# Layer 1 of an eight-expert network by seven block products: a graph-attention and expert-layer kernel in float32

## What is computed

```
x1  = x + gnn(layernorm(x), adj)                       # 128 graphs, softmax over 128 neighbours
xn  = layernorm(x1)
w   = softmax(mean over graphs(xn) @ Wr + br)          # [node, expert]
h   = relu(bn(xn @ W1[e] + b1[e]))                     # 256 x 256 each, bn = scale and shift
h   = relu(bn(h  @ W2[e] + b2[e]))
y   = sum over e of  w[node, e] * (h @ Wo[e] + bo[e])
out = x1 + y
```

## Time and profile before

| | before |
|---|---|
| three runs, us | 2537.67, 2536.6, 2537.84; median 2537.67 |
| span of the profiled execution, us | 2535.1 |
| PE busy, share of the span | 2453.0 us, 97% |
| ACT busy | 1592.8 us, 63% |
| DVE busy | 1479.0 us, 58% |
| POOL busy | 408.1 us, 16% |
| DMA | 116.02 MB, mean 46 GB/s |

### The profile page before, as it was taken

How to read it: one execution, slowest core, us unless ns; L and a number is a source line. 1 busy time by engine, 2 the same in 40 slices (tenths; PEclk the granted TensorE clock), 3 DMA queues, 4 the chain that set the end, 5 groups by cost and what they waited for, 6 DMA issues and landing times.

```text
span 2535.1 us, 38086 instructions
## 1 busy us (share of the span) xinstructions
PE 2453.0 (97%) x14000; PEld 2125.7 (84%) x14000; DVE 1479.0 (58%) x2160; ACT 1592.8 (63%) x2142; POOL 408.1 (16%) x450
## 2 busy tenths in 40 slices
PE   7888789999999999999999999999999999999998
PEld 6666668888888888888888888888888888888887
DVE  6999965555555555555555555555555555555554
ACT  6777746666666666666666666666666666666665
POOL 5888820000000000000000000000000000000000
PEclk9999989999999999999999999999999999999999
DMA  6666510000000000000000000000000000000000
GB/s 190 214 203 202 188 61 26 26 12 13 25 25 25 25 25 25 25 25 25 25 25 25 25 2 22 25 25 25 25 25 25 25 25 25 25 25 25 14 11 25
DMA packets 88991, 116.02 MB, mean 46 GB/s; under 512 B 4572, under 2 KB 76680, under 8 KB 88968
## 3 DMA queue, kind: packets, MB, share of 16 engines
...
## 4 chain that ended last, share of the span: by engine, by line
PE 86%; ACT 0%; DVE 0%; issue 0%
PE ps_wide L158 56%; PE ps_y L1096 28%; PE ps_t L145 1%; ACT h L923 0%; DVE h_lo L1003 0%; DVE h2w L998 0%; ACT h_hi L948 0%; DVE out_sb L1010 0%; ACT h_hi L935 0%; PE ps_t L1112 0%; ACT featT L958 0%; PE ps_t L1107 0%; DVE h_lo L991 0%
## 5 line engine op out<-in xcount | busy, mean ns | idle before, releaser
L923 ACT ACTIVATE h<-ps_wide,bn_cols 128x512 f32<-128x512 f32 x1024 | 791.0, 776 | 494.7 <-PE ps_wide L158 487.4
L991 DVE TENSOR_TENSOR h_lo<-h,h_hi 128x1024 fp32r<-128x1024 f32 x256 | 313.4, 1224 | 604.1 <-ACT h_hi L935 604.1
L1096 PE MATMUL ps_y<-w_hi,h_hi 128*128 128x256 f32 x2048 | 572.2, 279 | 2.2 <-DVE h_lo L1003 2.2
L1096 PE MATMUL ps_y<-w_lo,h_hi 128*128 128x256 f32 x2048 | 571.8, 279 | 0.0
L1096 PE MATMUL ps_y<-w_hi,h_lo 128*128 128x256 f32 x2048 | 570.8, 279 | 0.0
L1003 DVE TENSOR_TENSOR h_lo<-h2w,h_hi 128x1024 fp32r<-128x1024 f32 x256 | 376.5, 1471 | 290.7 <-ACT h_hi L948 290.7
L948 ACT ACTIVATE h_hi<-h2w 128x1024 fp32r<-128x1024 f32 x256 | 271.4, 1060 | 336.5 <-DVE h2w L998 336.5
L158 PE MATMUL ps_wide<-xT_hi,w_hi 128*128 128x512 f32 x1024 | 405.6, 396 | 3.3 <-ACT h L923 3.3
L158 PE MATMUL ps_wide<-h_hi,w_hi 128*128 128x512 f32 x1024 | 407.7, 398 | 0.0
L158 PE MATMUL ps_wide<-xT_lo,w_hi 128*128 128x512 f32 x1024 | 405.8, 396 | 0.0
L158 PE MATMUL ps_wide<-xT_hi,w_lo 128*128 128x512 f32 x1024 | 405.4, 396 | 0.0
...
## 6 DMA issues: line engine op xcount, KB each, us to landing
x_sb<-in_x SPq DMA_DIRECT2D x32, 512.0 KB, 3.5
res<-in_x SPq DMA_DIRECT2D x32, 512.0 KB, 4.5
x_scratch<-x SPq DMA_DIRECT2D x32, 512.0 KB, 3.0
x1t<-x_scratch SPq DMA_DIRECT2D x32, 512.0 KB, 4.5
resb<-x_scratch SPq DMA_DIRECT2D x32, 512.0 KB, 5.2
out<-out_sb SPq DMA_DIRECT2D x32, 512.0 KB, 3.6
...
```

The costliest lines, as they stand in the source:

```text
L923: last = nc.scalar.activation(h[:, c, :], psum[:, c, :], ACT.Relu, bias=bn_cols[:, row + 1, C * e + c:C * e + c + 1], scale=bn_cols[:, row ...
L991: nc.vector.tensor_tensor(h1_lo[p][:, :, :], h1[:, :, :], h1_hi[p][:, :, :].bitcast(F32), ALU.subtract).then_inc(lo1_done, 1)
L1096: mm = nc.tensor.matmul(ps_y[:, b4, :], h[:, c, cols], w[:, i, c, :], start=(e == 0 and n == 0 and b4 % per_bank == 0), stop=(e == E - 1 a ...
```

## The change

Layer 1 is computed by Strassen's scheme, in the form with shared sums: the 256 x 256 weight is four blocks of 128 x 128, x is four blocks of 128 x 256 (two feature halves by two halves of the 512 columns), and instead of eight block products there are seven. Each is three matmuls of 256 columns. Names: a tile's seven x blocks stand in `xs`, `xq_hi`, `xq_lo`, an expert's seven weight blocks in `wq_hi`, `wq_lo`.

- **Weight sums**, in the first stage: POOL makes four sums of 128 columns for an expert and the low part of 896 columns, ACT the high part, one expert in two groups; then W2 one a group. Wo is loaded and split in the second stage, at its start (`wo_hi`, `wo_lo`).
- **x sums**, once a tile: ACT copies the transposed x to `xs` (`tile_copy`), POOL makes four differences (`tile_sums`), and ACT and DVE split the seven blocks in three pieces of 3, 2 and 2 blocks (`tile_high`, `tile_low`).
- **Partial results**: PE accumulates product 1 (`a_sum`); ACT reads it with scale and shift into `v` (v1); PE adds products 4 and 5, ACT reads again (v2); PE adds product 6, ACT reads a third time (v3). DVE adds what the other half of the banks holds: `sum_2` writes z of output half 1 from v3, `sum_1` z of output half 0 from v1 and v2, after product 7. ACT's high part takes relu with it, and DVE's low part is max(z, 0) - high.
- **Order**: a step runs layer 1 of a unit, layer 2 of the unit before, and layer 3 of the unit three back (`LEAD = 3`), interleaved as below. There is one set of h1 parts in place of two, and h2 is gated in place.
- **Statistics kept**: the mean and reciprocal deviation of every group, which the first stage has for the feature mean anyway, stay in `mean_all` and `rstd_all`; the second stage no longer computes them. x is normalised in place in `x1t`.
- **Output**: the residual sum is made in `resb` itself in two halves, so the residual of the next tile is loaded after the store of this one has landed.

The diff, cut to its core:

```diff
+        def tile_copy(act, t, ps_x):
+            act.wait_ge(xT_ready, t + 1)
+            wait(act, xqlo_done, 3 * t)
+            for c, (first, step) in enumerate(((B11, B12 - B11), (B21, B22 - B21))):
+                last = nc.scalar.activation(xs[:, first:first + step + 1:step, :],
+                                            ps_x[:, c, :].rearrange("p (t n) -> p t n", n=H), ACT.Copy)
+            last.then_inc(xs_copied, 1)
+
+        def tile_sums(pool, t):
+            pool.wait_ge(xs_copied, t + 1)
+            nc.gpsimd.tensor_tensor(xs[:, T1, :], xs[:, B12, :], xs[:, B11, :], ALU.subtract).then_inc(xs_sum, 1)
+            nc.gpsimd.tensor_tensor(xs[:, T3, :], xs[:, B22, :], xs[:, B12, :], ALU.subtract).then_inc(xs_sum, 1)
+            pool.wait_ge(xs_sum, 4 * t + 2)
+            nc.gpsimd.tensor_tensor(xs[:, T2, :], xs[:, B22, :], xs[:, T1, :], ALU.subtract).then_inc(xs_sum, 1)
+            pool.wait_ge(xs_sum, 4 * t + 3)
+            nc.gpsimd.tensor_tensor(xs[:, T4, :], xs[:, B21, :], xs[:, T2, :], ALU.subtract).then_inc(xs_sum, 1)
+
+        def tile_high(act, t, group):
+            act.wait_ge(xs_sum, 4 * (t + 1))
+            q = slice(*X_GROUPS[group])
+            nc.scalar.activation(xq_hi[:, q, :], xs[:, q, :], ACT.Copy).then_inc(xqhi_done, 1)
...
-            def steps(t, last):
-                for s in range(1, E + 1):
-                    us = [unit(t, s + 2), unit(t, s + 1), unit(t, s)]
...
             @block.sync
...
+                    wait(sp, out_stored, 16 * t)
                     sp.dma_start(resb[:, :, :].rearrange("p b d -> p (b d)"), x1_dram[t]).then_inc(res_loaded_b, 16)
-                    sp.wait_ge(out_done, t + 1)
-                    sp.dma_start(out_g[t], out_sb[:, :, :]).then_inc(out_stored, 16)
+                    sp.wait_ge(out_done, 2 * (t + 1))
+                    sp.dma_start(out_g[t], resb[:, :, :]).then_inc(out_stored, 16)
...
             @block.scalar
...
+                def step(t, n):
+                    new, prev, old = unit(t, n), unit(t, n - 1), unit(t, n - 2)
+                    if exists_unit(prev):
+                        high_1(prev)
...
+                    if exists_unit(new):
+                        act.wait_ge(p1_done, uno(new) + 1)
+                        wait(act, z1_done, uno(new))
+                        copy_sum(new, 0, 0, v1_done)
+                    if exists_unit(old):
+                        relu_2(old, 1)
+                    if new[1] == E - 1 and exists_unit(unit(t, n + 1)):
+                        act.wait_ge(p2_done, uno(new) + 1)
+                        tile_high(act, unit(t, n + 1)[0], 0)
+                    if exists_unit(new):
+                        act.wait_ge(p4_done, uno(new) + 1)
+                        copy_sum(new, 1, 0, v2_done)
...
+                    if exists_unit(old):
+                        high_2(old)
+                    if new[1] == E - 1 and exists_unit(unit(t, n + 1)):
+                        tile_high(act, unit(t, n + 1)[0], 1)
+                    if exists_unit(new):
+                        act.wait_ge(p7_done, uno(new) + 1)
+                        wait(act, z2_done, uno(new))
+                        copy_sum(new, 2, 1, v3_done)
...
+                    if exists_unit(prev):
+                        relu_2(prev, 0)
+                    if new[1] == E - 2 and exists_unit(unit(t, n + 2)):
+                        tile_copy(act, unit(t, n + 2)[0], ps_t_x)
...
             @block.vector
...
+                def step(t, n):
+                    new, prev, old = unit(t, n), unit(t, n - 1), unit(t, n - 2)
+                    done = unit(t, n - LEAD)
+                    if exists_unit(prev):
+                        low_1(prev)
...
+                    if exists_unit(old):
+                        gate_2(old)
+                    if new[1] == E - 1 and exists_unit(unit(t, n + 1)):
+                        tile_low(dve, unit(t, n + 1)[0], 0)
+                    if done[1] == E - 1 and exists_unit(done):
+                        out_add(done[0], 0)
+                        out_add(done[0], 1)
+                    if exists_unit(new):
+                        sum_2(new)
+                    if exists_unit(old):
+                        low_2(old)
+                    if new[1] == E - 1 and exists_unit(unit(t, n + 1)):
+                        tile_low(dve, unit(t, n + 1)[0], 1)
+                    if exists_unit(new):
+                        sum_1(new)
...
             @block.tensor
...
+                def strassen(out_ps, e, q, start, stop):
+
+                    terms = ((wq_hi, xq_hi), (wq_lo, xq_hi), (wq_hi, xq_lo))
+                    for n, (w, x) in enumerate(terms):
+                        mm = nc.tensor.matmul(out_ps, w[:, e, q, :], x[:, q, :], start=start and n == 0,
+                                              stop=stop and n == len(terms) - 1, skip_group_check=True)
+                    return mm
...
+                        wait(pe, z2_done, uno(new))
+                        strassen(a_sum, e, 0, True, False).then_inc(p1_done, 1)
+                        wait(pe, z1_done, uno(new))
+                        strassen(x_p5, e, 1, True, False)
+                        strassen(x_p2, e, 2, False, False).then_inc(p2_done, 1)
...
+                        layer_3(done, 0)
+                    if exists_unit(new):
+                        pe.wait_ge(v1_done, uno(new) + 1)
...
+                        strassen(a_sum, e, 3, False, False)
+                        strassen(a_p4, e, 4, False, False).then_inc(p4_done, 1)
...
+                    if exists_unit(done):
+                        layer_3(done, 1)
+                    if exists_unit(new):
+                        pe.wait_ge(v2_done, uno(new) + 1)
...
+                        strassen(a_sum, e, 5, False, True).then_inc(p7_done, 1)
+                    if exists_unit(prev):
+                        pe.wait_ge(lo1_done, uno(prev) + 1)
+                        wait(pe, r2_done, C * uno(prev))
+                        layer_2(prev, 0)
+                    if exists_unit(new):
+                        pe.wait_ge(z2_done, uno(new) + 1)
+                        strassen(x_p5, e, 6, False, True).then_inc(p3_done, 1)
+                    if exists_unit(prev):
+                        layer_2(prev, 1)
```

656 lines of the change are left out of this document (347 added, 309 removed).

## The result

| | before | after |
|---|---|---|
| time, median of the runs (us) | 2537.76 | 2699.24 |
| range (us) | 2536.6 to 2538.99 | 2698.47 to 2699.66 |
| span of the profiled execution (us) | 2535.1 | 2697.5 |
| TensorE (PE) busy | 97% | 93% |
| tile in the expert stage (us) | 68.06 | 72.49 |

A forecast was written before the change was run, and what follows sets the result against it. It took PE's own queue to bound the expert stage. Its terms summed to +114 us on a span of 2535.1, so 2649, and 2652 us as the runs' median, 4.5% slower, with a range of 2575 to 2735.

The forecast's parts named there:

- hand-over: Between product 6 and product 7 in each unit: PE waits some 0.2 us for ACT and DVE, +45 us.
- the high ends: Upper bounds of the forecast's terms, which its range up to 2735 us had to take in.
- products: Layer 1 on PE: 21 matmuls of 256 columns replace 12 of 512, 0.35 us less a unit, -90 us.
- product 6 to product 7: Layer 1: ACT's read and DVE's sum outlast half of layer 2 by 0.2 us a unit, +45 us.
- step before a new tile: Once a tile, POOL's differences delay ACT's v2 and PE's products 6 and 7: 3.75 us in 31 tiles, +116 us.
- the piece ahead of the last sum: DVE's piece of x work adds a 0.2 us wait at the next step's second product, +6 us.
- rival 2: PE's clock falls after each tile's 2.9 us gap, 1.7 us lost each time, +54 us, 2706 us; chance 0.2.
- residual: Later residual load makes POOL's bias addition block DVE's low part of layer 2, 0.5 us a tile, +15 us.
- first stage and crossing: POOL's added weight work, +6 us, and a later barrier between the stages, +4 us.
- start of the second stage: First steps: feature mean, gate and third-layer weight splits stand between the hand-overs, +12 us.
- Rival 1: Expert stage: PE stays the bound, a tile takes about 66.9 us, 2523 us in all, faster; chance 0.11.
- rival 3: Expert stage: the loop of DVE and ACT rules every unit at 8.7 us, 2767 us; chance 0.07.

The follow-up runs named there:

- e2: The changed kernel with product 7 behind eight of layer 2's twelve matmuls instead of six: 2650.5 us.
- e12: e11 with DVE's third low piece of x put back behind the second, in the step of expert 7: 2493.4 us.
- e3: The changed kernel with 18 matmuls that nobody reads put ahead of product 6 in the step of expert 7: 2694.2 us.
- e1: The changed kernel with the next tile's normalisation, transposes, ACT's copies and POOL's four differences one step earlier: 2626.3 us.
- e4: e1 with the four differences of x made by DVE instead of POOL, behind its last sum in the step of expert 6: 2598.7 us.
- e5: e4 and e2 together: 2557.9 us.
- e10: e9 with the bias added to the residual by DVE in the step of expert 5 instead of by POOL: 2505.8 us.
- e11: e10 with third-layer weights split one expert a step, eight steps instead of four, and the first residual loaded earlier: 2502.5 us.
- e9: e5 with DVE's later low pieces one place later, and ACT's copies and second piece and DVE's differences moved into idle waits: 2524.9 us.

## Why the prediction was right, and where it was short

The mechanism was right: PE waits for DVE's z ahead of product 7, and once a tile for ACT's v behind POOL's differences. The sum of the terms was +114 us against a span of 2535.1; it came to +162.4. The two largest errors, of PE's own work (21 us) and of the hand-over (24), lie on the same side, so the range holds through the room that it left for the clock and the high ends.

| term, as predicted | predicted | measured | from |
|---|---|---|---|
| products | -90 | -69 | plain step with all waits gone, 8.13 (e2, e12), against 8.40: 0.27 x 256 |
| product 6 to product 7 | +45 | +69 | 8.44 - 8.13 = 0.31, x 224 |
| step before a new tile | +116 | +116 | 11.87 - 8.13 = 3.74, x 31 |
| the piece ahead of the last sum | +6 | +9 | step 0 without low clock 8.73 (e3), less 8.44, x 31 |
| clock (rival 2) | 0 | +7 | 8.94 - 8.73, x 31 |
| residual | +15 | +4 | 8.58 - 8.44, x 31 |
| first stage and crossing | +10 | +5 | 351.49 - 346.80 |
| start of the second stage | +12 | +20 | what is left of 162.4 |
| tail | 0 | +2 | 6.6 - 4.6 |

**Products.** The step "half the columns cost half the time" was wrong by a little, and 256 times over. I took 0.117 us for 256 columns from 24 halves in a row behind 24 whole ones. In a step where 45 of 57 matmuls have 256 columns, 8.13 less 12 times 0.233 leaves 0.1184 for each. That is 0.08 us a unit, 21 us in all. In e12, where nothing waits, it lies with layer 3 as well: its two halves of 12 matmuls take 1.43 us each, 2.86 together, where its 24 in a row took 2.80 before, and the 21 of the products take some 2.49 instead of 2.45. So "nothing else leaves PE" was right, and that what stays keeps its price was not. One half in e12, its first matmul and the product's behind it, 1.43 us apart:

```profile
1252.14 0.28 PE L1201 MATMUL ps_y<-wo_hi,h_hi 128*128 128x256 f32 x1
...
1253.57 0.28 PE L1181 MATMUL ps_wide<-xq_hi,wq_hi 128*128 128x256 f32 x1
```

Why 256-column matmuls are some 1.5% slower in this order was not tried.

**Product 6 to product 7.** Five of the six parts fit: 0.32 from product 6's last matmul to ACT (0.31 charged), 0.60 from there to DVE (0.58). The sum takes 0.75 us and not 0.67; I had taken the fastest of 32 of another line, with both operands in SBUF, where the same row has a median of 1.42; both new sums, the one over two banks of PSUM (L1069, 751 ns on average) and the one over one (L1079, 744), take longer than that. With 0.04 more at the hops and the restart, 0.31 instead of 0.2 us: +24. e2 shows that it is this wait, and that nothing takes its place in a plain step.

**The step before a new tile.** Right in the sum, 3.74 against 3.75, which is in part luck: the forecast's own parts, 2.9 to 3.0 and 0.95, make 3.9, and the 0.2 of the 0.95 that it left out as usual is in no other term, since that of the hand-over takes only seven units. Its tile of 71.4 us is not the sum of its terms either; these give 71.1. In its parts: the four differences take 4.8 us from first to last (4.9 forecast), product 6 loses 2.53 and 0.10 at its restart (2.9 to 3.0), product 7 0.69 and 0.10 in e3, where no low clock blurs it (0.95). The last 0.3 us of the 3.74 I can't place. That POOL and DVE hold each other up is there (1.60 and 1.62 us for 0.74 and 1.23), though not for every pair: POOL's second difference took 0.74 us with DVE's operation begun 0.20 behind it. e1 takes 3.28 us off step 7 and leaves 0.93 to the blocking, which e4 removes. By my halving of the earlier trace rows a difference was 0.65; it takes 0.72 to 0.74 alone. By the Trainium skill's 2.6 cycles an element (GPSIMD Engine Reference, section 3.1) I had estimated 0.56. From 256 to 512 columns the time grows by 0.54 us (0.73 to 1.27 in the earlier trace rows), so the slope agrees with the page; what neither its cycles an element nor my halving priced is the 0.19 us that an operation costs beside its elements.

**Residual.** The blocking came (1.79 instead of 1.22 us), in a step with enough slack: 0.14 us a tile instead of 0.5. Once e2 had taken the slack out, the same blocking cost 0.5, as e5's and e10's step 4 show. A bound worked out for a kernel with no slack would have been right for e5 and was wrong here.

**First stage and crossing.** PE's last eight matmuls of the attention begin at 338.23 against 337.26, so in these two traces the first stage cost 1.0 us of the 6 forecast, and the crossing the other 3.7, where I had 4. The start differs by up to 3 us among the runs with the new kernel's first stage, so this term is no surer than that.

**Start.** Two things were not charged at all. The first unit's layer 1 now comes behind the barrier, 2.5 us by my own price for it. And the clock is low behind the crossing, before for nine matmuls and now for longer; the stretch from 360 to 370 us, first before, then after:

```profile
360.00:370.00 10.00, 8.59 (x50) 6.94 (x50) 6.04 (x5) 5.39 (x9) 0.00 (x0) 1.00 0.01 2
```

```profile
360.00:370.00 10.00, 9.35 (x36) 7.65 (x35) 6.63 (x10) 4.08 (x8) 1.97 (x3) 0.56 0.17 52
```

At a granted clock of 0.56 that is at most 4.4 us of PE's work (0.44 times 10, an estimate). Three things stretch tile 0 to 84.7 us and were charged too low together: DVE's gate beside POOL's first bias addition (3.4 us for 1.22), DVE's low part beside POOL's third-layer weights (2.20 for 1.23), and the gate's chain.

```profile
394.54 2.20 DVE L1086 SCALAR_TENSOR_TENSOR h_lo<-z,h_hi 128x1024 fp32r<-128x1024 f32 x1 [2.23 <-ACT h_hi L987]
396.67 3.42 DVE L1093 TENSOR_TENSOR h<-h,w_bc 128x1024 f32<-128x1024 f32 x1
```

```profile
393.12 2.55 POOL L963 TENSOR_TENSOR wo_lo<-w_stage,wo_hi 128x512 fp32r<-128x512 f32 x2 [7.15 <-ACT wo_hi L1057]
395.62 3.39 POOL L970 TENSOR_TENSOR resb<-resb,bias_out 128x1024 f32<-128x1024 f32 x1
```

e10 and e11 take 4.7 us from the first tile (e9's 80.1 to 75.4). The rest, 9 us over a later tile of e11, stays open between the gate's own chain and PE's half clock at the crossing.

**Rivals.** Rival 1 (PE stays the bound) had a tile of 66.9 us; that is what e9 to e12 reach (66.79 to 66.02), by another order of the same work and with DVE in POOL's place. Rival 2 (the clock) came in half of the tiles and cost 0.2 us a tile, not the 1.7 that I charged; its sign, 256-column matmuls twice as far apart, stands in these tiles (1231.07 and 1231.29 us in the one shown above, 0.22 instead of 0.12). The Trainium skill (TensorE: Matmul & The Clock Gate, section on HAM oscillation) tells of a kernel that waits for a DMA in each tile, for longer than PE does here, and begins every tile at half rate. With gaps of 2.4 us about half did (14 of 29, in e2 21 of 30), and e3 gives the price. What would have shown the forecast wrong, steps over 8.5 us throughout (rival 3), did not come: 8.44, and the cause of the 0.31 was the hand-over.
